# An expert stage on one core: token lists two groups earlier, a row buffer of their own, the third hidden transpose moved back, and the next rows' splits queued behind weight splits

## The reference

```
scores = softmax(x2d @ gate_w.T); top 2 of 8 experts for each of the 512 tokens
xr     = token's row * its score, tokens sorted by expert
h      = silu(xr @ w1[e]) * (xr @ w3[e])      # w1, w3: 512 x 1408
out   += h @ w2[e]                            # w2: 1408 x 512
```

## Time and profile before

| | us |
|---|---|
| median of 3 runs | 1936.03 (1935.92 to 1937.83) |
| the profiled execution's own time | 1930.54 |
| its span, first to last instruction | 1929.2 |
| PE busy | 1762.4 (91%) |
| DVE busy | 1248.4 (65%) |
| ACT busy | 948.7 (49%) |
| POOL busy | 443.3 (23%) |
| expert loop, first XG matmul to last | 1572.2 to 1911.7 |

### The profile page before, as it was taken

One profiled execution on the slowest core, in us unless ns is written; L12 is line 12 of the kernel. 1 busy time (PEld: TensorE's weight loads), 2 busy tenths in 40 slices (PEclk: granted clock), 3 DMA queues, 4 the chain that ended last, 5 costly groups with the idle time before them and its releaser, 6 DMA issues.

```text
span 1929.2 us, 25864 instructions
## 1 busy us (share of the span) xinstructions
PE 1762.4 (91%) x9438; PEld 1438.9 (75%) x9438; DVE 1248.4 (65%) x2521; ACT 948.7 (49%) x1969; POOL 443.3 (23%) x262
## 2 busy tenths in 40 slices
PE   6889999997999889999999999998888869889896
PEld 4667787875878679999899988886455547768785
DVE  5888989884543426667677767996434356665753
ACT  4454545452243225556566656885222345565552
POOL 1444546451000012113111211221111012221221
PEclk9999999998999999999999999999999879999998
DMA  6122222113720399778677767676300346685721
GB/s 232 66 87 88 88 88 88 69 63 131 270 75 1 104 283 318 234 231 244 195 237 221 239 193 201 183 222 225 131 6 6 121 152 231 239 286 187 259 75 61
DMA packets 147134, 310.03 MB, mean 161 GB/s; under 512 B 11472, under 2 KB 100816, under 8 KB 135440
## 3 DMA queue, kind: packets, MB, share of 16 engines
q1 hardware_dynamic: 145072, 301.85, 47.7%
q0 software_dynamic: 1920, 6.36, 1.0%
HBM read 226.88 MB, written 81.28 MB: 160 GB/s over the span
## 4 chain that ended last, share of the span: by engine, by line
PE 68%; DVE 21%; ACT 5%; DMA 3%; issue 2%; DVEq 0%; POOL 0%; ACTq 0%; SPq 0%; POOLq 0%
PE bank L101 11%; PE bank L102 10%; PE bank L103 10%; PE bank L1089 4%; PE bank L1629 4%; PE bank L1630 4%; PE bank L1633 4%; PE bank L1311 3%; DVE PTL L1096 2%; PE bank L1044 2%; DVE TT L1046 2%; PE bank L1115 2%; PE bank L1116 2%; DVE CNL L426 2%; DVE FA L340 2%
## 5 line engine op out<-in xcount | busy, mean ns | idle before, releaser
L1096 DVE TENSOR_TENSOR PTL<-bank,PTH 128x512 fp32r<-128x512 f32 x256 | 176.0, 688 | 95.0 <-ACT PTH L1094 93.6
L1094 ACT CAST PTH<-bank 128x512 fp32r<-128x512 f32 x256 | 149.9, 586 | 165.1 <-PE bank L1089 165.1
L1616 DVE TENSOR_TENSOR WS<-EW,WS 128x1024 fp32r<-128x1024 f32 (+1 forms) x120 | 150.5, 1264 | 70.8 <-ACT WS L1613 70.4
L1074 ACT ACTIVATE TT<-TT,MX 128x512 f32<-128x512 f32 x256 | 186.5, 729 | 8.6 <-DVE MX L1064 8.6
L1046 DVE CUSTOM_DVE_ANT_0 TT<-bank,MASK 128x512 f32<-128x512 f32 x256 | 174.3, 682 | 8.7 <-POOL MASK L1027 6.6
L1613 ACT CAST WS<-EW 128x1024 fp32r<-128x1024 f32 (+1 forms) x144 | 139.3, 977 | 48.6 <-PE bank L1633 44.2
L1089 PE MATMUL bank<-IDN,TT 128*128 128x128 f32 x1024 | 155.2, 274 | 4.0 <-DVE RS L1139 2.9
L101 PE MATMUL bank<-BCH,WKT 128*128 128x256 f32 x512 | 149.7, 292 | 4.8 <-DVE BCL L608 4.1
L102 PE MATMUL bank<-BCL,WKT 128*128 128x256 f32 x512 | 146.0, 285 | 0.0
L103 PE MATMUL bank<-BCH,WKT 128*128 128x256 f32 x512 | 146.0, 285 | 0.0
L466 POOL TENSOR_TENSOR KS<-KS,FH 128x512 f32<-128x512 f32 x60 | 100.7, 1678 | 197.2 <-DVE FL L456 197.1
(11 more groups left out here) (291 smaller groups left out, 4598.4 us busy)
## 6 DMA issues: line engine op xcount, KB each, us to landing
EW<-in_ewg SPq DMA_DIRECT2D x48, 1024.0 KB, 5.3
KST<-tmp_k SPq DMA_DIRECT2D x43, 768.0 KB, 5.8
tmp_k<-EKH SPq DMA_DIRECT2D x128, 256.0 KB, 2.8
EW<-in_ewg SPq DMA_DIRECT2D x24, 768.0 KB, 4.2
CT<-in_ctxT SPq DMA_DIRECT2D x32, 512.0 KB, 4.4
CN<-in_ctxN SPq DMA_DIRECT2D x32, 512.0 KB, 3.4
BCT<-in_ctxT SPq DMA_DIRECT2D x32, 512.0 KB, 3.4
tmp_k<-EKL SPq DMA_DIRECT2D x64, 256.0 KB, 2.9
```

The source lines that it names most:

```text
L1074: t_e[(n, kc)] = tick("act", act.activation(TT[:, sl, cs], TT[:, sl, cs], ACT.Exp, bias=MX[:, n % 4, 5:6], scale=SC1, accum_out=SUM[:, b % ...
L1096: t = free[bk] = tick("dve", dve.tensor_tensor(PTL[:, q], bank[bk][:], f(PTH[:, q]), ALU.subtract))
L1616: t_lo = tick(low, E[low].tensor_tensor(WS[:, s, 1, 0:n * w], src, f(WS[:, s, 0, 0:n * w]), ALU.subtract))
```

## The change

Seven edits, all in the expert stage:

1. `gather_act` writes, and `turn_pe` reads, a buffer of its own, HX, in place of HS. LB moves into EW[0], and `back` waits for the last reader of EW[0].
2. Block 0's group 3 uses bank 4 in place of bank b.
3. `pick` follows groups 0 and 1, the lists are made in groups 2 and 3, both in bank 5.
4. `hidden_zero(2)` moves from behind half 12 to behind half 13.
5. `gather_act(0)` moves ahead of half 13; `gather_act(1)` behind half 14 and its split.
6. `turn_pe(0)` stays behind half 14; `turn_act(0)` moves behind the split that follows; `turn_dve(0)`, and with it block 1's `turn_pe` and `turn_act`, move behind half 15 and its split.
7. Block 1's `turn_dve` moves behind half 16 and its split.

```
+        HX = [R(f"HX{v}", [128, 512]) for v in range(2)]
...
         def gather_act(e, v):
-            need("act", T[v]["hg"], T[v]["hs"])
+            need("act", T[v]["hg"], T[v]["hx"])
             T[v]["xw"] = T[v]["hgr"] = tick(SEM[v]["act"], act.activation(
-                HS[v][:], HG[v][:, 0:512], ACT.Copy, scale=HG[v][:, 512 + e:513 + e]))
+                HX[v][:], HG[v][:, 0:512], ACT.Copy, scale=HG[v][:, 512 + e:513 + e]))
...
-        LB = [R(f"LB{i}", [128, 512]) for i in range(4)]
+        LB = [EW[0][:, 512 * i:512 * i + 512] for i in range(4)]
...
-            need("pool", t_fin, T[0]["yo"], T[1]["yo"])
+            need("pool", t_fin, T[0]["yo"], T[1]["yo"], *ew_read[5 * NE])
...
             for g in range(6):
                 n, wi = divmod(g, 2)
-                bk, bk1 = (b, b1) if wi else (a, a1)
+                bk, bk1 = (4 if g == 3 else b, b1) if wi else (a, a1)
                 group_one(e, g, bk1)
                 nxt = half_zero(e, g, 0, bk)
                 if wi and n:
                     hidden_zero(n - 1, 7)
-                if g in (4, 5) and not last:
-                    list_tokens(g - 4, g + 1)
+                if g in (2, 3) and not last:
+                    list_tokens(g - 2, 5)
                 split_half(nxt)
...
-                if g in (2, 3) and not last:
-                    pick(e + 1, g - 2)
+                if g in (0, 1) and not last:
+                    pick(e + 1, g)
...
             group_one(e, 6, a1)
             nxt = half_zero(e, 6, 0, a)
-            hidden_zero(2, 7)
-            split_half(nxt)
-            nxt = half_zero(e, 6, 1, a)
             split_half(nxt)
             if not last:
                 gather_act(e + 1, 0)
-                when("act", e + 1, lambda: gather_act(e + 1, 1), ("act1",))
+            nxt = half_zero(e, 6, 1, a)
+            hidden_zero(2, 7)
+            split_half(nxt)
             group_one(e, 7, a1)
             nxt = half_zero(e, 7, 0, a)
             if not last:
                 turn_pe(0, 5, "pe")
-                turn_act(0, 5)
-                turn_dve(0, 5)
             split_half(nxt)
             if not last:
+                when("act", e + 1, lambda: gather_act(e + 1, 1), ("act1",))
+                turn_act(0, 5)
+            nxt = half_zero(e, 7, 1, a)
+            split_half(nxt)
+            if not last:
+                turn_dve(0, 5)
                 when("pe", e + 1, lambda: turn_pe(1, 6, "peg"), ("peg",))
                 when("act", e + 1, lambda: turn_act(1, 6), ("act1",))
-                when("dve", e + 1, lambda: turn_dve(1, 6), ("dve1",))
-            nxt = half_zero(e, 7, 1, a)
-            split_half(nxt)
             group_one(e, 8, a1)
             nxt = half_zero(e, 8, 0, a)
             split_half(nxt)
+            if not last:
+                when("dve", e + 1, lambda: turn_dve(1, 6), ("dve1",))
             nxt = half_zero(e, 8, 1, a)
```

More of the change, by code:

```diff
@@ L1644, in build @@
         SEM = [{"pe": "pe", "act": "act", "dve": "dve"}, {"pe": "pe1", "act": "act1", "dve": "dve1"}]
-        T = [dict.fromkeys(("gs", "hs", "ht", "yo", "xg", "xgr", "w", "pick", "hg", "hgr"), None) for _ in range(2)]
+        T = [dict.fromkeys(("gs", "hs", "hx", "ht", "yo", "xg", "xgr", "w", "pick", "hg", "hgr"), None) for _ in range(2)]
         for v in range(2):
@@ L1676, in turn_pe @@
             for c in range(4):
-                m = pe.transpose(bank[bk][:, 128 * c:128 * c + 128], HS[v][:, 128 * c:128 * c + 128], IDN[:])
-            T[v]["hs"] = T[v]["xwt"] = tick(sem, m)
+                m = pe.transpose(bank[bk][:, 128 * c:128 * c + 128], HX[v][:, 128 * c:128 * c + 128], IDN[:])
+            T[v]["hx"] = T[v]["xwt"] = tick(sem, m)
         def turn_act(v, bk):
@@ L1811, in build @@
         t_fin = tick("dve", dve.tensor_scalar(FIN[:, 0:4], KFT[:, 8:12], -1.0, None, ALU.add))
-        LB = [R(f"LB{i}", [128, 512]) for i in range(4)]
-        assert R.at <= io_at, (R.at, io_at)
+        LB = [EW[0][:, 512 * i:512 * i + 512] for i in range(4)]
         HB = [Region(yt_at + 2048 * i)(f"HB{i}", [128, 512]) for i in range(4)]
@@ L1818, in back @@
         def back(i):
-            need("pool", t_fin, T[0]["yo"], T[1]["yo"])
+            need("pool", t_fin, T[0]["yo"], T[1]["yo"], *ew_read[5 * NE])
             t_lb[i] = tick("lb", pool.indirect_dma_start(
-                LB[i][:], None, YD, bass.IndirectOffsetOnAxis(ap=FIN[:, i:i + 1], axis=0)), 16)
+                LB[i], None, YD, bass.IndirectOffsetOnAxis(ap=FIN[:, i:i + 1], axis=0)), 16)
         for e in range(8):
```

## The result

| | before | changed |
|---|---|---|
| median of the runs, us | 1936.03 (5 runs, 1935.81 to 1941.93) | 1945.6 (5 runs, 1945.17 to 1947.97) |
| profiled execution, own time | 1930.54 | 1945.41 |
| its span | 1929.2 | 1944.1 |
| expert loop in it | 339.4 | 355.0 |

The change makes the kernel slower: ratio 1.0041, 95% interval 1.0024 to 1.0058. The forecast was 1941.7 us, with a range of 1931 to 1949. "Expert loop" is the stretch from the first to the last matmul of the experts in the trace. Of the two profiled executions that of before is a quick one (5.5 us under its median), that of the changed kernel lies at its median; their loops differ by 15.5 us, the medians by 9.6.

A forecast was written before the change was run, and what follows sets the result against it. PE bounds two-block experts, a chain through several engines one-block ones. Terms summed to +2.3 us, +5.7 with the clock; added to the median 1936.03 that gave 1941.7 us, range 1931 to 1949.

The forecast's parts named there:

- rival A: Expert stage: XG's new place eats the middle's win, clock falls at two or more entries; 1937 to 1949 us, chance 0.52.
- XG behind the weights' splits: Expert ends: PE idle 3.0 us at half 16, 2.3 before a two-block expert's first group.
- Bank 4: Group 3: removes group 3's and 5's gate waits, 0.61 and 1.66 us, read as DVE lateness.
- Lists and third transpose: One-block experts' middle: half 11 ends at 18.6 us, not 21.5; with the later transpose 5.0 us won each.
- GS beside POOL: One-block experts: first GS group meets POOL's split, 0.8 us lost in each, bounds 0.3 to 1.1.
- The lower bound's case: First GS group in one-block experts: POOL waits for DVE, 0.3 us lost in each.
- The clock: Falls at two of three entries to two-block experts cost 3.4 us; those of experts 0 and 2 go, 1.6 won.
- forecast sign: Profile after the change: expert 2, a one-block expert, takes less than 32 us.
- The comparison: Whole kernel: loss summed on the profiled execution, 1930.54 us, then added to the runs' median, 1936.03, giving 1941.7.
- C: One-block experts' middle wins more than walked, making the kernel faster; 1929 to 1936 us, chance 0.24.
- D: One-block experts: POOL's queue becomes the bound, both gathers taking 2.83 us; 1950 us, chance 0.08.

The follow-up runs named there:

- e1: Changed kernel with edits 6 and 7 undone (next rows' turn, cast and split again ahead of the weight splits): 1924.6 us, ratio 0.9912 to 0.9960.
- e2: Kernel before with edits 6 and 7 alone (next rows' turns moved behind the weight splits): 1955.3 us, ratio 1.0067 to 1.0126.
- e6: e1 without bank 4, group 3 of block 0 using bank b again: 1921.0 us, ratio 0.9907 to 0.9944.
- e7: e1 with the lists where they were (pick behind groups 2 and 3, lists in groups 4 and 5): 1935.9 us, ratio 0.9990 to 1.0021.
- e4: Changed kernel plus 60 matmuls nobody reads, placed inside PE's idle times: 1937.3 us, ratio 0.9988 to 1.0023.
- e3: Changed kernel with PE waiting in each expert only for the token of that expert's own rows: 1932.4 us, ratio 0.9960 to 0.9995.
- e5: e1 and e3 together (edits 6 and 7 undone, PE waiting for its own expert's rows only): 1916.6 us, ratio 0.9871 to 0.9911.
- e8: e1 with the third transpose behind half 12 again: 1933.7 us, ratio 0.9974 to 0.9996.
- e10: Changed kernel with edit 7 alone undone (block 1's XG split ahead of group 8 again): 1942.5 us, ratio 1.0020 to 1.0049.

## Why the prediction was right

The direction, the range and the main cause held: it was rival A, with falls at all four entries. That the number came within 3.9 us is in part luck. The sum was made on a profiled execution, and against that one it said 5.7 where the changed profile has 15.5 more. By its steps:

- *XG behind the weights' splits.* Right, and the sizes too. Forecast 3.0 idle at half 16 with a one-block successor, measured 3.00; with a two-block successor PE has turned block 1 meanwhile, measured 2.56 to 2.62; 2.3 before a two-block expert, measured 2.10 to 2.38. Too high only in two-block experts: 1.0 forecast, 0.3 to 0.5 measured. Sum 24 against 21.1. e1 and e2 show that this step carries the loss.
- *Bank 4.* "DVE lateness, not a lack of banks" is confirmed by e6. The waits went because DVE's work moved, not because of the bank.
- *Lists and third transpose.* Forecast was the end of half 11 at 18.6 us from the start of expert 5, not 21.5. Measured from first matmul to the first of group 6: 18.4 (1785.63 to 1804.02), before 21.5 (1779.00 to 1800.49). The 3 us won are right, their parts were not: the 1.0 us of waiting at half 11 for POOL shrank to 0.2 (the gathers held POOL 2.30 and 1.41 us, forecast were 2.83 and 1.68), and 0.56 went to list 0, below. POOL's split held DVE's instead: two splits took 4.24 where they need 2.4, and the 1.84 more are as long as POOL's split. Gate 2 made PE wait 1.5 to 1.6 where 0.8 was forecast; that the one comes of the other is my reading. The two terms together, 1.8, were about right. (e7 against e1, 13.8 over four experts, is no measure of the forecast's 3 us: it is mostly clock.) DVE, then POOL, in expert 5:

```profile
1801.50 4.24 DVE L1617 TENSOR_TENSOR WS<-EW,WS 128x1024 fp32r<-128x1024 f32 x2
```

```profile
1801.66 1.84 POOL L1617 TENSOR_TENSOR WS<-EW,WS 128x768 fp32r<-128x768 f32 x1
```

- *GS beside POOL.* Both cases exist, depending on a few tenths. In expert 3 POOL's split began 0.71 us after the first GS instruction, and the four took their 0.87; in expert 5 it began 0.33 after it, the four took 3.02, and PE lost 0.56 at the list. The lower bound's case, in which POOL waits for DVE, did not come. 0.8 in each expert was too much: two of four were caught, experts 2 and 5, at 0.6 of PE each. DVE in experts 3 and 5, then POOL's splits in the same experts:

```profile
1703.15 0.87 DVE L1655 TENSOR_SCALAR GS<-IO,POS 128x128 fp32r<-128x128 f32 x4
...
1790.08 3.02 DVE L1655 TENSOR_SCALAR GS<-IO,POS 128x128 fp32r<-128x128 f32 x4
```

```profile
1703.86 2.43 POOL L1617 TENSOR_TENSOR WS<-EW,WS 128x1024 fp32r<-128x1024 f32 x1 [14.59 <-ACT WS L1614]
...
1790.41 2.41 POOL L1617 TENSOR_TENSOR WS<-EW,WS 128x1024 fp32r<-128x1024 f32 x1 [13.50 <-ACT WS L1614]
```

This agrees with the Trainium skill, GPSIMD Engine Reference, section 8 (Key points), on the SBUF interfaces shared with VectorE, but who comes first is decided by the schedule.
- *The clock.* This is the term that was mis-sized. Net +1.8 was forecast (two falls of 1.7, two of 0.8 taken away). Measured: six falls more, 23.9 us more at half clock, at e4's 0.41 about 9.8 us. That is 8.0 over the forecast, of the 9.8 by which the loop's 15.5 are over 5.7. A fall came behind each of the four waits of 2.1 to 2.4 and, in three of four one-block experts, behind or around the chain of 1.5 and 3.0; I had taken two of three at the entries and none elsewhere. Expert 2 shows it best: its forecast sign, under 32 us, failed outright. It took 35.6, at a mean clock of 0.88, and its idle times sum to less than before (5.1 against 5.4). The price of a fall in a one-block expert was low too: 0.8 came from windows of unequal offset, from first matmul to first matmul expert 2 took 1.1 more than expert 5.
- *The comparison.* The sum was made against a profiled execution that lay 5.5 us under the median of its runs. Against that one the loss is 15.5, against the medians 9.6. Executions of one kernel differ by their clock: in the 25 runs of the kernel before that were measured beside e1 to e4 (1923.9 to 1943.8 us) the time rises by 0.41 us with each us at half clock that their mean granted clock implies (0.970 in the quickest, 0.960 in the slowest; correlation 0.94). Part of it stands ahead of the loop, where the twelve traces differ by 10 us with the same code. Both profiled executions reached the loop early, at 1572.2 and 1571.5; the middle of the twelve is 1575.6. With that as the start, the medians as the ends and 17.6 us behind the loop in both traces I estimate loops of 341.5 before and 351 changed, so before's was 2 us quick and the changed one's 4 us slow. In which stages the other executions had their falls is not shown.

The rivals C and D did not come. The middle won about 4.6 in expert 3, not the 5.0 of the forecast and far from C's 8: its first half starts at 1698.42, half 15's last two matmuls at 1724.94, 26.5 against 30.2 before (1809.18 from 1779.00, expert 5), and 0.9 of those 26.5 are the clock's, from the fall that reaches into the expert's start.

## What to carry to other kernels

A wait that names the latest token of a double-buffered tile also waits for the next user's data: keep the token of the own iteration (e3 and e5 won 13 and 8 us by it). It does not make every reordering free: with the own token edits 6 and 7 still cost 16 us (e3 against e5), since block 1's rows came too late in earnest. Before a step is queued behind others, follow what frees the slot of those others: here each split waited for the very matmuls that stood in front of the consumer, so the chain could never be hidden. And where PE's idle times come near 2 us, price a fall of the clock behind them, above all when the stage behind is bound by PE, and judge by several executions, since the falls differ from one to the next.

## What was not expected of the hardware

The forecast gave the clock 1.8 us net; e4 shows that it took more than the added idle time in the changed kernel (11 us of loop for 27 us at 1.2 GHz, with 4.8 us of idle time added over before), and that useless matmuls in a wait are cheaper than the wait. The waits of 2.1 to 2.4 us before a two-block expert, twelve in three kernels (changed, e2, e3), were all followed by a fall, while of those of 1.4 us standing alone (e1, e6) none was. Those of 1.5 to 1.7 went both ways, and longer ones were no surer than 2.4: of the 23 waits of 2.5 to 3.2 us in the loops of the changed kernel, e2, e7, e8 and e10, 17 had a fall within them or less than 1 us behind. Of the six without, five (three in e2, two in the changed kernel) were followed within 5 us by one of 2.4, and that one had the fall; the sixth is e10's 3.2. What decides it stays open.
